# A decoder layer's cross attention: three of six score units get their exponentials head by head on ScalarE

## The chip, the cores and the metric

The kernel runs on one NeuronCore of a Trainium2 chip. A core has engines that run side by side, each with its own instruction stream in fixed order: TensorE (PE, matrix products into PSUM), VectorE (DVE), ScalarE (ACT), GpSimd (POOL) and the queue engine SyncE (SP), which here only issues DMAs. They meet through semaphores. The metric is the device time of the whole program in microseconds (us).

## What is computed

One post-norm decoder layer in float32 for 32 batches of 112 tokens, width 256, 16 heads of 16; the context has 375 tokens per batch. The part that matters here is the cross attention. Its softmax runs over axis 1, the queries, and not over the context:

```python
q = (queries @ Wq + bq).reshape(N, L, H, D)
k = (keys @ Wk + bk).reshape(N, S, H, D)
v = (values @ Wv + bv).reshape(N, S, H, D)
sm = jnp.einsum('nlhd,nshd->nlhs', q, k) / math.sqrt(D)
sm = jax.nn.softmax(sm, axis=1)
attn = jnp.einsum('nlhs,nshd->nlhd', sm, v).reshape(N, L, H * D)
return attn @ Wo + bo
...
x = _layernorm(x + self_attention(x))
x = _layernorm(x + cross_attention(x, ctx, ctx))
x = _layernorm(x + ffn(x))
```

So for each context token and head there is a maximum over 112 queries, an exponential of (score - maximum), and a sum over the same 112 queries.

## The kernel before, in words

The program has three parts one after the other: the feed-forward weights are quantised, then `attention` treats the 32 batches (self attention, cross attention, two layer norms), then the feed-forward part runs over all batches. The change is in `attention`.

**Pipeline.** The batches go through a software pipeline of seven stages. One step of each engine's program works on up to seven batches, n0 (oldest) to n6 (newest). The steps run from i = -6 to 31; in the 26 steps i = 0 to 25 all stages are present (22 of them in a hardware loop of 11 pairs). The order inside a step is written out by hand for each engine, in the functions `step` under `block.tensor`, `block.vector`, `block.scalar` and `block.gpsimd`.

**Units.** The cross scores of one batch are six units, C0 to C5: unit u = (t, c) takes eight heads (t = 0 or 1) and a third of the context (125 tokens, c = 0 to 2). A unit is a tile of 125 partitions (context tokens) by 8 heads x 112 queries = 896 columns, in one of two PSUM slots `score`. `SLOT_USES` fixes the turn: slot 0 takes C4, C5, C1, C2; slot 1 takes S1, C0, S0, C3 (S0 and S1 are the self attention's scores). `wait_slot` makes PE wait until the exponentials of the slot's previous tenant are done.

**A unit's way through the engines**, before:

1. PE `cross_scores` (L1062): six matmuls (L1002).
2. DVE `max_cross` (L744): negated maximum per head, 125x8, into `nmax_c` (L747).
3. PE `transpose_max` (L1071): `nmax_c` transposed into the PSUM tile `maxT` (L1074).
4. ACT `copy_max` (L564): copy to `nmaxT` (L567).
5. PE `shift` (L1076): two selector matmuls add the negated maxima onto the scores in PSUM (L1080).
6. ACT `exp_cross` (L558): one exponential over 125x896 (L561) into `Px`.
7. DVE `sum_cross` (L725): the sums per head into `Zc` (L729); `reciprocal_cross` (L731), then `normalise_values` (L735), which multiplies the values by the reciprocals into `Vn` (L740).
8. PE `cross_values` (L1084): products into `outX` (L1091).

The self attention goes another way: `exp_self` (L546) takes eight exponentials of 112x112, one per head, each with its own bias (the negated maximum) and the sum in ACT's accumulator (L554).

**Around the change.** In an ACT step, `even_cross` (L623, on `outX` after C5's products) stands ahead of `exp_cross(n3, 1)`, behind which come `even_self(n4, 1)` and `exp_self(n5, 0)`. `copy_x1T` stands ahead of `exp_cross(n3, 3)`, and `hi_queries_cross` (tile `Qx_hi`, L573) behind it. On DVE `lo_with_bias` (L758, `Qx_lo`, L763) follows `Qx_hi`; on POOL `block_diagonal` (L482, `Qbd` and `Kbd`, L485) follows that, in a fixed order with `inverse_root` (L503, `rstd`, L506), which needs DVE's `add_eps` (L837, `vare`, L839). In the PE steps the order is: output projection of n0, self keys, shift of C3, ..., C4, ..., S1, ..., C5, ..., C0, ..., transposed maxima of C0, ..., C1, ..., products of C5, ..., C2, ..., C3, ..., transposed maxima of C3.

Of the kernel before, what the change touches and what calls it, by code (L numbers as in the profile page):

```python
# [33 lines left out]
SP = S + 1  # L34
NU = KT * NC
QW = QUAD * L
HALF_ROWS = QUAD * HD
# [52 lines left out]
class Batch:  # L90
# [21 lines left out]
    def loads(self):  # L112

        fixed = 16 * (self.off // 2 + 1)
        return self.pair * 16 + fixed if self.looped else fixed

    def first_fills(self, use):
# [207 lines left out]
def attention(nc, a, ident, x2T_all, xmax_all, x2_dram, constants):  # L325
    with ExitStack() as ctx:
# [38 lines left out]
        x1b = [sb(f"x1b{p}", [L, D]) for p in range(2)]  # L365
        nmax_c = [sb(f"nmax_c{p}", [C, P]) for p in range(2)]
        nmaxT = [sb(f"nmaxT{p}", [P, SP // NC + 1], F32R) for p in range(2)]
        Px = [sb(f"Px{p}", [C, OCT, L]) for p in range(2)]
# [30 lines left out]
        scores_c, nmax_c_done, nmaxT_done = sem("scores_c"), sem("nmax_c_done"), sem("nmaxT_done")  # L399
        nmaxT_copied, shifted, exp_c = sem("nmaxT_copied"), sem("shifted"), sem("exp_c")  # L400
        z_c, rz_c, vn_done, av_done = sem("z_c"), sem("rz_c"), sem("vn_done"), sem("av_done")
# [136 lines left out]
        def _(act):  # L538
# [18 lines left out]

            def exp_cross(n, u):  # L558
                act.wait_ge(shifted, n.times(NU, u + 1))
                wait(act, av_done, n.times(NU, u - 1))  # L560
                act.activation(Px[u % 2][:].rearrange("s (q h) l -> s q (h l)", q=2),  # L561
                               score[SLOT_OF[f"C{u}"]][0:C, :, 0:QW], ACT.Exp).then_inc(exp_c, 1)

            def copy_max(n, u):  # L564
                act.wait_ge(nmaxT_done, n.times(NU, u + 1))
                wait(act, shifted, n.times(NU, u - 1))
                act.activation(nmaxT[u % 2][:, 0:C], maxT[:, 0:C], ACT.Copy).then_inc(nmaxT_copied, 1)  # L567

# [72 lines left out]
            def step(n0, n1, n2, n3, n4, n5, n6):  # L641
                if n4:
                    copy_probs(n4, 0)
                if n2:
                    copy_max(n2, 4)
                    exp_cross(n2, 4)
# [7 lines left out]
                if n2:  # L654
                    copy_max(n2, 5)
                if n4:
                    copy_probs(n4, 2)
                    hi_context(n4, 0)
                if n2:
                    exp_cross(n2, 5)  # L660
                if n3:
                    copy_max(n3, 0)
                if n4:
                    even_self(n4, 0)
                if n3:
                    exp_cross(n3, 0)
                if n4:
                    hi_context(n4, 1)
                    copy_probs(n4, 3)
                if n3:  # L670
                    copy_max(n3, 1)
                if n1:
                    copy_x2T(n1)
                if n2:
                    even_cross(n2)
                if n3:
                    exp_cross(n3, 1)
                if n4:
                    even_self(n4, 1)
                if n5:  # L680
                    exp_self(n5, 0)
                if n3:
                    copy_max(n3, 2)
                if n4:
                    hi_keys_cross(n4, 0)
                if n3:
                    exp_cross(n3, 2)
# [4 lines left out]
                if n3:  # L692
                    copy_max(n3, 3)
                if n6:
                    hi_keys_self(n6)
                if n4:
                    copy_x1T(n4)
                if n3:
                    exp_cross(n3, 3)
                if n4:  # L700
                    hi_queries_cross(n4)
# [3 lines left out]
        def _(dve):  # L705
# [38 lines left out]
            def max_cross(n, u):  # L744
                dve.wait_ge(scores_c, n.times(NU, u + 1))
                wait(dve, nmaxT_done, n.times(NU, u - 1))
                dve.tensor_reduce(nmax_c[u % 2][:, 0:OCT].rearrange("s (q h) -> s q h", q=2),  # L747
                                  score[SLOT_OF[f"C{u}"]][0:C, :, 0:QW].rearrange("s q (h l) -> s q h l", h=QUAD),
                                  AX.X, ALU.max, negate=True).then_inc(nmax_c_done, 1)

# [110 lines left out]
            def step(n0, n1, n2, n3, n4, n5, n6):  # L861
# [9 lines left out]
                if n3:  # L871
                    normalise_values(n3, 2)
                    max_cross(n3, 4)
                    sum_cross(n3, 3)
                if n5:
# [30 lines left out]
                if n5:  # L906
                    lo_context(n5, 0)
                if n3:
                    sum_cross(n3, 5)
                if n5:  # L910
# [31 lines left out]
                if n5:  # L942
                    residual(n5, 0)
                if n4:
                    sum_cross(n4, 1)
                if n5:
# [20 lines left out]
        def _(pe):  # L967
# [103 lines left out]
            def transpose_max(n, u):  # L1071
                pe.wait_ge(nmax_c_done, n.times(NU, u + 1))
                wait(pe, nmaxT_copied, n.times(NU, u))
                pe.transpose(maxT[:, 0:C], nmax_c[u % 2][:], ident[0:C, 0:C]).then_inc(nmaxT_done, 1)  # L1074

            def shift(n, u):  # L1076

                pe.wait_ge(nmaxT_copied, n.times(NU, u + 1))
                for q in range(2):
                    ins = pe.matmul(score[SLOT_OF[f"C{u}"]][0:C, q, 0:QW], nmaxT[u % 2][:, 0:C],  # L1080
                                    sel[:, q * QW:(q + 1) * QW], start=False, stop=True, skip_group_check=True)
# [59 lines left out]
            def step(n0, n1, n2, n3, n4, n5, n6):  # L1141
                if n0:
                    project_out_cross(n0)
                if n4:
                    project_T(n4, "Ks", w["aWk"], xT, "xT")
                if n1:
                    shift(n1, 3)
                if n2:
# [23 lines left out]
                if n4:  # L1172
                    project_T(n4, "Qs", w["aWq"], xT, "xT")
                if n1:
                    transpose_max(n1, 5)
# [5 lines left out]
                if n1:  # L1181
                    shift(n1, 5)
                if n3:
# [12 lines left out]
                if n4:  # L1196
                    self_scores(n4, 0)
                if n2:
                    transpose_max(n2, 1)
# [4 lines left out]
                if n2:  # L1204
                    shift(n2, 1)
                if n3:
# [19 lines left out]
                if n2:  # L1226
                    cross_values(n2, 1)
                    transpose_max(n2, 3)
            iterations(pe, step)


# [606 lines left out]
```

## Time and profile before

| what | value |
|---|---|
| time, median of 3 runs (lowest to highest) | 1400.16 us (1396.43 to 1400.56) |
| time of the profiled execution | 1398.15 us |
| its span in the profile | 1396.4 us |
| busy share of the span: PE, DVE, ACT, POOL | 88%, 83%, 62%, 28% |

The shares are over the whole program. A stage's own limit is read from a stretch of it: each engine's busy time there, then what each engine waits for at the places where it does wait, and the start times of one step side by side. A row of the timeline gives an instruction's start and duration, and in brackets how long the engine was idle ahead of it and who released it. Back-to-back instructions of one engine overlap in the rows, so the time that one takes from its engine is the distance from its start to the next one's start, which is shorter than its duration.

### The profile page before, as it was taken

The numbers are of one execution on the slowest core, as the hardware profiler recorded it, in microseconds if no ns is written. First come the engines' busy times: TensorE is split into PE (matmuls) and PEld (weight loads), VectorE is DVE, ScalarE is ACT, GpSimd is POOL, SyncE is SP. The second block draws the span as 40 slices with busy tenths as digits, with TensorE's granted clock in tenths as the row PEclk, the third lists the DMA queues.
The fourth block names the chain that finished last, engine by engine and source line by source line (L and its number), as shares of the span: only waits on it lengthen the run. The fifth ranks groups of instructions, "written<-read, shape, count | busy, mean of one in ns | idle before, by whom it ended". The sixth has DMA issues, their size and how long they took to land. (4 is left out here: it accounts for less than half of the span.)

```text
span 1396.4 us, 28360 instructions
## 1 busy us (share of the span) xinstructions
PE 1226.5 (88%) x8850; PEld 897.2 (64%) x8850; DVE 1159.4 (83%) x2358; ACT 859.7 (62%) x2306; POOL 396.4 (28%) x463
## 2 busy tenths in 40 slices
PE   1689999999999999999999999999858878596776
PEld 1466666666666666666666666666527766496776
DVE  6369999999999999999999999999853468868787
ACT  2366666666666666666666666666424479786443
POOL 0233322234322234322234322233100000000887
PEclk9999999999999999999999999999969989798898
DMA  5100000000000000000000000000000000000222
GB/s 159 39 19 16 19 28 25 18 21 18 18 27 22 18 21 18 18 28 21 18 21 18 18 29 21 19 19 5 7 7 1 0 0 0 0 1 8 62 69 72
DMA packets 35042, 33.07 MB, mean 24 GB/s; under 512 B 4148, under 2 KB 34604, under 8 KB 34988
## 3 DMA queue, kind: packets, MB, share of 16 engines
q1 hardware_dynamic: 32704, 31.50, 7.3%
q10 hardware_dynamic: 2284, 0.89, 0.3%
q8 instruction: 30, 0.49, 0.1%
q14 instruction: 24, 0.20, 0.0%
HBM read 25.04 MB, written 7.34 MB: 23 GB/s over the span
## 5 line engine op out<-in xcount | busy, mean ns | idle before, releaser
L561 ACT ACTIVATE Px<-score 125x896 f32<-125x896 f32 x192 | 176.2, 918 | 128.1 <-PE score L1080 66.7
L747 DVE TENSOR_REDUCE nmax_c<-score 125x8 f32<-125x896 f32 x192 | 208.3, 1085 | 5.6 <-PE score L1002 5.1
L729 DVE TENSOR_REDUCE Zc<-Px 125x8 f32<-125x896 f32 x192 | 206.6, 1076 | 7.3 <-ACT Px L561 3.8
L554 ACT ACTIVATE Ps<-score,nmax_s 112x112 f32<-112x112 f32 x512 | 173.1, 377 | 3.9 <-DVE nmax_s L754 3.9
L506 POOL TENSOR_TENSOR rstd<-vare,half 112x1 f32<-112x1 f32 x64 | 35.1, 548 | 473.6 <-DVE vare L839 473.6
L1080 PE MATMUL score<-sel,nmaxT 128*125 128x448 f32 x384 | 125.1, 407 | 1.8 <-ACT nmaxT L567 1.8
L554 ACT ACTIVATION_READ_ACCUMULATOR Ps<-score,nmax_s 112x1 f32 x512 | 118.6, 232 | 0.0
L1091 PE MATMUL outX<-Px,Vn 125*32 125x224 f32 x1536 | 113.2, 368 | 2.5 <-DVE Vn L740 2.5
L740 DVE TENSOR_TENSOR Vn<-Vx,rZc 125x128 f32<-125x128 f32 x192 | 112.8, 588 | 1.2
L567 ACT ACTIVATE nmaxT<-maxT 128x125 fp32r<-128x125 f32 x192 | 53.5, 279 | 89.2 <-PE maxT L1074 88.9
L1002 PE MATMUL score<-Qbd_hi,KxT_hi 64*125 64x448 f32 x384 | 90.3, 466 | 1.2 <-ACT Px L561 1.2
L485 POOL TENSOR_TENSOR Qbd_hi<-Qx_hi,mask 128x448 fp32r<-128x448 f32 x64 | 59.7, 933 | 103.2 <-DVE Qx_lo L763 102.2
L1074 PE MATMUL maxT<-ident,nmax_c 125*128 125x125 f32 x192 | 59.7, 311 | 31.2 <-DVE nmax_c L747 31.2
L593 ACT ACTIVATE PsT<-work 112x448 f32<-112x448 f32 x128 | 69.5, 543 | 25.9 <-PE work L1126 24.5
L1126 PE MATMUL work<-ident,Ps 112*112 112x112 f32 x512 | 75.5, 270 | 3.6 <-ACT Ps L554 2.0
L1074 PEld LDWEIGHTS maxT<-ident,nmax_c 125*128 125x128 f32 x192 | 27.3, 142 | 79.6 <-DVE nmax_c L747 57.4
L1126 PEld LDWEIGHTS work<-ident,Ps 112*112 112x112 f32 x512 | 51.5, 134 | 36.4 <-DVE KxT_lo L776 10.1
L1080 PEld LDWEIGHTS score<-sel,nmaxT 128*125 128x125 f32 x384 | 57.5, 187 | 24.9 <-ACT nmaxT L567 17.4
L754 DVE TENSOR_REDUCE nmax_s<-score 112x8 f32<-112x896 f32 x64 | 69.1, 1080 | 3.3 <-PE score L1002 3.3
L1002 PE MATMUL score<-Qbd_hi,KxT_lo 64*125 64x448 f32 x384 | 71.2, 364 | 0.0
L1002 PE MATMUL score<-Qbd_lo,KxT_hi 64*125 64x448 f32 x384 | 71.1, 365 | 0.0
L1667 POOL MEMSET fhalf<- 112x1 f32 x1 | 0.1, 98 | 249.6 <-POOLq L1544 249.6
(252 smaller groups left out, 3588.1 us busy)
## 6 DMA issues: line engine op xcount, KB each, us to landing
ctx_in<-in_ctx SPq DMA_DIRECT2D x32, 375.0 KB
x_in<-in_x SPq DMA_DIRECT2D x32, 112.0 KB, 2.0
x_scratch<-x SPq DMA_DIRECT2D x32, 112.0 KB, 5.4
x2T_all<-x_scratch SPq DMA_DIRECT2D x32, 112.0 KB, 2.0
out<-x2T_all SPq DMA_DIRECT2D x32, 112.0 KB, 1.9
raw_w_up<-in_w_up SPq DMA_DIRECT2D x1, 768.0 KB, 5.6
raw_w_down<-in_w_down SPq DMA_DIRECT2D x1, 768.0 KB, 7.2
raw_w_gate<-in_w_gate SPq DMA_DIRECT2D x1, 768.0 KB, 9.6
```

The source lines that it names most:

```text
L554: ins = act.activation(Ps[:, g, :], score[slot][0:L, h // QUAD, (h % QUAD) * L:(h % QUAD + 1) * L], ACT.Exp, bias=nmax_s[:, g:g + 1], accu ...
L561: act.activation(Px[u % 2][:].rearrange("s (q h) l -> s q (h l)", q=2), score[SLOT_OF[f"C{u}"]][0:C, :, 0:QW], ACT.Exp).then_inc(exp_c, 1)
L593: act.activation(dst, work[b][0:rows_, 0:cols], ACT.Copy).then_inc(drained[b], 1)
L729: dve.tensor_reduce(Zc[p][:], Px[p][:], AX.X, ALU.add).then_inc(z_c, 1)
L740: dve.tensor_tensor(Vn[p][:], Vx[n.par][:, c, P * t:P * (t + 1)].rearrange("s (h e) -> s h e", h=OCT), rZc[p][:].rearrange("s (h o) -> s h ...
L747: dve.tensor_reduce(nmax_c[u % 2][:, 0:OCT].rearrange("s (q h) -> s q h", q=2), score[SLOT_OF[f"C{u}"]][0:C, :, 0:QW].rearrange("s q (h l) ...
L754: dve.tensor_reduce(nmax_s[:, OCT * t:OCT * (t + 1)].rearrange("s (q h) -> s q h", q=2), score[SLOT_OF[f"S{t}"]][0:L, :, 0:QW].rearrange(" ...
L1002: ins = pe.matmul(dst[:, q, 0:QW], lhs[a][rows, t, cols], rhs[b][rows, t].rearrange("p h l -> p (h l)"), start=(first and i == 0), stop=(i ...
L1074: pe.transpose(maxT[:, 0:C], nmax_c[u % 2][:], ident[0:C, 0:C]).then_inc(nmaxT_done, 1)
L1080: ins = pe.matmul(score[SLOT_OF[f"C{u}"]][0:C, q, 0:QW], nmaxT[u % 2][:, 0:C], sel[:, q * QW:(q + 1) * QW], start=False, stop=True, skip_g ...
L1091: ins = pe.matmul(outX[32 * g:32 * (g + 1), t, :], Vn[u % 2][:, 2 * g:2 * g + 2, :].rearrange("s h e -> s (h e)"), Px[u % 2][:, 2 * g:2 * ...
L1126: ins = pe.transpose(b[0:L, h * L:(h + 1) * L], Ps[:, QUAD * j + h, :], ident[0:L, 0:L])
```

## The change

The units are split: C1, C3 and C5 (`BY_HEAD`) lose the steps 3, 4, 5 and the DVE sum, and their exponentials are eight ACT instructions of 125x112, one per head, with the negated maximum as bias and the sum in the accumulator (`exp_by_head`). C0, C2 and C4 (`SHIFTED`) go as before. The maxima of the by-head units go to tiles of their own (`nmax_h`); counts and buffer parities of the shifted units follow their own numbering. The by-head exponentials stand where the single ones stood. Nothing else is reordered.

```diff
+BY_HEAD = (1, 3, 5)
+SHIFTED = tuple(u for u in range(NU) if u not in BY_HEAD)
...
+            def exp_by_head(n, u):
+                i = BY_HEAD.index(u)
+                act.wait_ge(nmax_h_done, n.times(NBH, i + 1))
+                wait(act, av_done, n.times(NU, u - 1))
+                maxima, sums = nmax_h[(n.par * NBH + i) % 2], Zc[u % 2]
+                for h in range(OCT):
+                    ins = act.activation(Px[u % 2][:, h, :],
+                                         score[SLOT_OF[f"C{u}"]][0:C, h // QUAD, (h % QUAD) * L:(h % QUAD + 1) * L],
+                                         ACT.Exp, bias=maxima[:, h:h + 1], accum_out=sums[:, h:h + 1])
+                ins.then_inc(exp_c, 1)
...
             def reciprocal_cross(n, u):
-                dve.wait_ge(z_c, n.times(NU, u + 1))
+                if u in BY_HEAD:
+                    dve.wait_ge(exp_c, n.times(NU, u + 1))
+                else:
+                    dve.wait_ge(z_c, n.shifts(SHIFTED.index(u) + 1))
...
-                if n3:
-                    copy_max(n3, 1)
                 if n1:
                     copy_x2T(n1)
                 if n2:
                     even_cross(n2)
                 if n3:
-                    exp_cross(n3, 1)
+                    exp_by_head(n3, 1)
```

The other two copies on ACT, the sums of units 1, 3 and 5 on DVE (three lines), and their transposes and shifts on PE (three of each) are taken out of the steps in the same way.

On ACT, the stretch around unit 1's exponential, before (`work` is a PSUM bank, L554 is `exp_self`, L626 `even_cross`):

```order
L567 ACTIVATE nmaxT1<-maxT 128x125
L433 REGISTER_ALU
L604 ISA
L604 ACTIVATE x2T_all<-work1 128x2x112
L142 REGISTER_ALU
L626 ACTIVATE evenX<-outX,even_odd 128x224
L561 ACTIVATE Px1<-score0 125x896
L433 REGISTER_ALU
L620 ACTIVATE evenT<-work0,even_odd 128x112
L548 REGISTER_ALU
L554 ACTIVATE Ps,Zs<-score1,nmax_s 112x112 x8
```

and the same stretch after:

```order
L631 ISA
L631 ACTIVATE x2T_all<-work1 128x2x112
L651 REGISTER_ALU
L155 REGISTER_ALU
L653 ACTIVATE evenX<-outX,even_odd 128x224
L579 ACTIVATE Px1,Zc1<-score0,nmax_h0 125x112 x8
L447 REGISTER_ALU
L647 ACTIVATE evenT<-work0,even_odd 128x112
L562 REGISTER_ALU
L568 ACTIVATE Ps,Zs<-score1,nmax_s 112x112 x8
```

The copy of the maxima is gone, and one instruction between `evenX` and `evenT` has become eight. On PE, the stretch from the output projection (`xWo`) to C4's first product, before:

```order
L1039 MATMUL work<-xWo,OxT 112x256 x2
L142 ISA
L1031 MATMUL work<-xT,aWk 128x112 x4
L1078 ISA
L1080 MATMUL score<-sel,nmaxT 125x448 x2
L1019 REGISTER_ALU
L142 REGISTER_ALU
L1011 MATMUL work<-ident,x 128x112 x2
L142 REGISTER_ALU
L1002 MATMUL score<-Qbd_hi,KxT_hi 125x448 x2
```

and after:

```order
L1065 MATMUL work<-xWo,OxT 112x256 x2
L155 ISA
L1057 MATMUL work<-xT,aWk 128x112 x4
L1045 REGISTER_ALU
L155 REGISTER_ALU
L1037 MATMUL work<-ident,x 128x112 x2
L155 ISA
L1028 MATMUL score<-Qbd_hi,KxT_hi 125x448 x2
```

C3's shift has gone from between the self keys and the transpose of x1; the rest stands in the same order.

## Rows read from the trace of the kernel before

**Rows 1.** Busy time of the engines in three stretches; x is the count, PEclk the granted clock.

```profile
core 0: us, PE busy (x) PEld busy (x) DVE busy (x) ACT busy (x) POOL busy (x), PEclk, DMA share, GB/s
400.00:600.00 200.00, 193.73 (x1546) 132.73 (x1546) 186.76 (x408) 134.24 (x436) 67.31 (x83) 1.00 0.07 21
980.00:1010.00 30.00, 25.67 (x197) 15.94 (x189) 26.85 (x59) 13.41 (x29) 5.48 (x7) 1.00 0.02 6
```

**Rows 2.** Timeline of PE, one step; start, duration, engine, line, instruction, idle before.

```profile
517.59 1.03 PE L1039 MATMUL work<-xWo,OxT 128*112 128x256 f32 x4
...
519.26 0.65 PE L1080 MATMUL score<-sel,nmaxT 128*125 128x448 f32 x2
519.75 0.36 PE L1011 MATMUL work<-ident,x 112*128 112x112 f32 x2
...
533.09 0.33 PE L1074 MATMUL maxT<-ident,nmax_c 125*128 125x125 f32 x1 [0.86 <-DVE nmax_c L747]
...
534.16 0.66 PE L1080 MATMUL score<-sel,nmaxT 128*125 128x448 f32 x2
...
537.46 0.59 PE L1091 MATMUL outX<-Px,Vn 125*32 125x224 f32 x8
...
540.10 0.46 PE L1002 MATMUL score<-Qbd_hi,KxT_hi 64*125 64x448 f32 x2
...
547.29 0.33 PE L1074 MATMUL maxT<-ident,nmax_c 125*128 125x125 f32 x1
547.45 1.03 PE L1039 MATMUL work<-xWo,OxT 128*112 128x256 f32 x4
```

**Rows 3.** Timeline of DVE: C3's sum.

```profile
542.40 1.08 DVE L729 TENSOR_REDUCE Zc<-Px 125x8 f32<-125x896 f32 x1
```

**Rows 4.** The page's group for the copies; busy us, mean ns of one, idle before.

```profile
L567 ACT ACTIVATE nmaxT<-maxT 128x125 fp32r<-128x125 f32 x192 | 53.5, 279 | 89.2 <-PE maxT L1074 88.9
```

**Rows 5.** Timeline of ACT: first and last head of `exp_self`, and on to C5.

```profile
526.02 0.35 ACT L554 ACTIVATE Ps<-score,nmax_s 112x112 f32<-112x112 f32 x1
...
528.58 0.24 ACT L554 ACTIVATION_READ_ACCUMULATOR Ps<-score,nmax_s 112x1 f32 x1
528.67 0.61 ACT L638 ACTIVATE KxT_hi<-work,xbk 128x375 fp32r<-128x375 f32 x1
...
531.60 0.92 ACT L561 ACTIVATE Px<-score 125x896 f32<-125x896 f32 x1
```

**Rows 6.** Timeline of ACT at the exponentials of C1.

```profile
538.20 0.45 ACT L626 ACTIVATE evenX<-outX,even_odd 128x224 f32<-128x224 f32 x1 [0.17 <-PE outX L1091]
538.69 0.92 ACT L561 ACTIVATE Px<-score 125x896 f32<-125x896 f32 x1
```

**Rows 7.** Timeline of ACT around the exponentials of C3.

```profile
519.53 0.60 ACT L573 ACTIVATE Ks_hi<-work,abk 128x112 fp32r<-128x112 f32 x2 [1.47 <-PE work L1031]
520.15 0.36 ACT L593 ACTIVATE x1T<-work 128x224 f32<-128x224 f32 x1
520.40 0.91 ACT L561 ACTIVATE Px<-score 125x896 f32<-125x896 f32 x1
522.38 0.60 ACT L573 ACTIVATE Qx_hi<-work,xbq 128x112 fp32r<-128x112 f32 x2 [1.07 <-PE work L1031]
```

**Rows 8.** Timeline of DVE behind `Qx_hi`.

```profile
523.88 0.96 DVE L740 TENSOR_TENSOR Vn<-Vx,rZc 125x128 f32<-125x128 f32 x1
524.76 1.08 DVE L754 TENSOR_REDUCE nmax_s<-score 112x8 f32<-112x896 f32 x1
...
530.40 1.63 DVE L740 TENSOR_TENSOR Vn<-Vx,rZc 125x128 f32<-125x128 f32 x1
```

**Rows 9.** Timeline of POOL behind `Qx_lo`.

```profile
523.76 0.93 POOL L485 TENSOR_TENSOR Qbd_hi<-Qx_hi,mask 128x448 fp32r<-128x448 f32 x1 [3.18 <-DVE Qx_lo L763]
...
525.98 0.55 POOL L506 TENSOR_TENSOR rstd<-vare,half 112x1 f32<-112x1 f32 x1 [0.35 <-DVE vare L839]
...
530.95 0.93 POOL L485 TENSOR_TENSOR Qbd_lo<-Qx_lo,mask 128x448 fp32r<-128x448 f32 x1
```

More of the change, by code:

```diff
@@ L35 @@
 NU = KT * NC
+BY_HEAD = (1, 3, 5)
+SHIFTED = tuple(u for u in range(NU) if u not in BY_HEAD)
+NSH = len(SHIFTED)
+NBH = len(BY_HEAD)
 QW = QUAD * L
@@ L115, in loads, with shifts, exps @@
         return self.pair * 16 + fixed if self.looped else fixed
+    def shifts(self, i):
+        return self.times(NSH, i)
+    def exps(self, place):
+        ahead, i = divmod(place, NBH)
+        return self.times(NU, NU * ahead + BY_HEAD[i] + 1)
     def first_fills(self, use):
@@ L366, in attention @@
         nmax_c = [sb(f"nmax_c{p}", [C, P]) for p in range(2)]
+        nmax_h = [sb(f"nmax_h{p}", [C, OCT]) for p in range(2)]
         nmaxT = [sb(f"nmaxT{p}", [P, SP // NC + 1], F32R) for p in range(2)]
@@ L399, in attention @@
         scores_c, nmax_c_done, nmaxT_done = sem("scores_c"), sem("nmax_c_done"), sem("nmaxT_done")
-        nmaxT_copied, shifted, exp_c = sem("nmaxT_copied"), sem("shifted"), sem("exp_c")
+        nmaxT_copied, shifted, exp_c, nmax_h_done = (sem(n) for n in ("nmaxT_copied", "shifted", "exp_c", "nmax_h_done"))
         z_c, rz_c, vn_done, av_done = sem("z_c"), sem("rz_c"), sem("vn_done"), sem("av_done")
@@ L556, in exp_self, with exp_shifted @@
                 ins.then_inc(exp_s, 1)
-            def exp_cross(n, u):
-                act.wait_ge(shifted, n.times(NU, u + 1))
+            def exp_by_head(n, u):
[8 more added lines that the diff above has]
+                ins.then_inc(exp_c, 1)
+            def exp_shifted(n, u):
+                act.wait_ge(shifted, n.shifts(SHIFTED.index(u) + 1))
                 wait(act, av_done, n.times(NU, u - 1))
@@ L564, in copy_max @@
             def copy_max(n, u):
-                act.wait_ge(nmaxT_done, n.times(NU, u + 1))
-                wait(act, shifted, n.times(NU, u - 1))
-                act.activation(nmaxT[u % 2][:, 0:C], maxT[:, 0:C], ACT.Copy).then_inc(nmaxT_copied, 1)
+                i = SHIFTED.index(u)
+                act.wait_ge(nmaxT_done, n.shifts(i + 1))
+                wait(act, shifted, n.shifts(i - 1))
+                act.activation(nmaxT[(n.par * NSH + i) % 2][:, 0:C], maxT[:, 0:C], ACT.Copy).then_inc(nmaxT_copied, 1)
             def hi_with_bias(n, use, dst, bias, done):
@@ L645, in step @@
                     copy_max(n2, 4)
-                    exp_cross(n2, 4)
+                    exp_shifted(n2, 4)
                 if n4:
@@ L659, in step @@
                 if n2:
-                    exp_cross(n2, 5)
+                    exp_by_head(n2, 5)
                 if n3:
@@ L665, in step @@
                 if n3:
-                    exp_cross(n3, 0)
+                    exp_shifted(n3, 0)
                 if n4:
@@ L686, in step @@
                 if n3:
-                    exp_cross(n3, 2)
+                    exp_shifted(n3, 2)
                 if n5:
@@ L691, in step @@
                     copy_xT(n6)
-                if n3:
-                    copy_max(n3, 3)
                 if n6:
@@ L698, in step @@
                 if n3:
-                    exp_cross(n3, 3)
+                    exp_by_head(n3, 3)
                 if n4:
@@ L745, in max_cross @@
                 dve.wait_ge(scores_c, n.times(NU, u + 1))
-                wait(dve, nmaxT_done, n.times(NU, u - 1))
-                dve.tensor_reduce(nmax_c[u % 2][:, 0:OCT].rearrange("s (q h) -> s q h", q=2),
+                if u in BY_HEAD:
+                    i = BY_HEAD.index(u)
+                    wait(dve, exp_c, n.exps(i - 2))
+                    dst, done = nmax_h[(n.par * NBH + i) % 2][:], nmax_h_done
+                else:
+                    i = SHIFTED.index(u)
+                    wait(dve, nmaxT_done, n.shifts(i - 1))
+                    dst, done = nmax_c[(n.par * NSH + i) % 2][:, 0:OCT], nmax_c_done
+                dve.tensor_reduce(dst.rearrange("s (q h) -> s q h", q=2),
                                   score[SLOT_OF[f"C{u}"]][0:C, :, 0:QW].rearrange("s q (h l) -> s q h l", h=QUAD),
-                                  AX.X, ALU.max, negate=True).then_inc(nmax_c_done, 1)
+                                  AX.X, ALU.max, negate=True).then_inc(done, 1)
             def max_self(n, t):
@@ L873, in step @@
                     max_cross(n3, 4)
-                    sum_cross(n3, 3)
                 if n5:
@@ L1071, in transpose_max @@
             def transpose_max(n, u):
-                pe.wait_ge(nmax_c_done, n.times(NU, u + 1))
-                wait(pe, nmaxT_copied, n.times(NU, u))
-                pe.transpose(maxT[:, 0:C], nmax_c[u % 2][:], ident[0:C, 0:C]).then_inc(nmaxT_done, 1)
+                i = SHIFTED.index(u)
+                pe.wait_ge(nmax_c_done, n.shifts(i + 1))
+                wait(pe, nmaxT_copied, n.shifts(i))
+                pe.transpose(maxT[:, 0:C], nmax_c[(n.par * NSH + i) % 2][:], ident[0:C, 0:C]).then_inc(nmaxT_done, 1)
             def shift(n, u):
-                pe.wait_ge(nmaxT_copied, n.times(NU, u + 1))
+                i = SHIFTED.index(u)
+                pe.wait_ge(nmaxT_copied, n.shifts(i + 1))
                 for q in range(2):
-                    ins = pe.matmul(score[SLOT_OF[f"C{u}"]][0:C, q, 0:QW], nmaxT[u % 2][:, 0:C],
+                    ins = pe.matmul(score[SLOT_OF[f"C{u}"]][0:C, q, 0:QW], nmaxT[(n.par * NSH + i) % 2][:, 0:C],
                                     sel[:, q * QW:(q + 1) * QW], start=False, stop=True, skip_group_check=True)
@@ L1145, in step @@
                     project_T(n4, "Ks", w["aWk"], xT, "xT")
-                if n1:
-                    shift(n1, 3)
                 if n2:
@@ L1180, in step @@
                     transpose_ctx(n3, 0)
-                if n1:
-                    shift(n1, 5)
                 if n3:
@@ L1203, in step @@
                     cross_values(n1, 5)
-                if n2:
-                    shift(n2, 1)
                 if n3:
@@ L1227, in step @@
                     cross_values(n2, 1)
-                    transpose_max(n2, 3)
             iterations(pe, step)
```

10 lines of the change are left out of this document (removed).

## The prediction

> **What bounds the kernel now.** I read the stretches first [rows 1]: from 400 to 600 us PE is busy for 193.7 of 200 us, DVE for 186.8 and ACT for 134.2, and PE has the full clock. Then the timeline of one PE step [rows 2]: PE waits for another engine at one place, 0.86 us for the maxima of C0. So a step is PE's own work plus that one wait. It is 29.86 us long, from the output projection at 517.59 to the next at 547.45. I cut it where the change can bite: **A** from the output projection to C0's transposed maxima (533.09), 15.50 us; **B** from there to the products of C5 (537.46), 4.37 us; **C** to the first matmul of C2 (540.10), 2.64 us; **D** to the next output projection, 7.35 us [rows 2].
>
> **What the change takes away.** On PE a shift is worth 519.75 - 519.26 = 0.49 us and a transposition of maxima 547.45 - 547.29 = 0.16 us [rows 2]; three of each are 1.95 us per step. On DVE a sum lasts 1.08 us [rows 3]; neighbours overlap, so I take 1.0 us, three are 3.0 us. ACT loses three copies of 0.28 us [rows 4]. If PE's work were all that counts, the step would fall to 27.9 us.
>
> **What it adds.** The nearest thing to the new exponentials is `exp_self`: eight heads of 112 columns, bias from a tile, sum in the accumulator, source in PSUM. From the first head to the next other instruction it takes 528.67 - 526.02 = 2.65 us of ACT, and its result is complete at 528.58 + 0.24 = 528.82, 2.80 us after the start [rows 5]. One exponential over the whole tile is complete 0.92 us after its start [rows 6]. So per by-head unit the exponentials end 1.88 us later from the same start. The new heads differ in having 125 partitions for 112; I take the same time for both. As a check of the total: ACT was busy for 134.2/200 x 29.86 = 20.0 us per step [rows 1]; three times (2.65 - 0.9) more, less three copies, gives about 25 us. ACT still has room on average, so its total is not the limit. What counts is where the longer blocks stand in its fixed order, and who waits behind them.
>
> Here the skill speaks for a lower price. By the row, head follows head every 2.65/8 = 0.33 us [rows 5]. The Trainium skill, page "ScalarE: Activation LUTs", section "What ACT_TABLE_LOAD costs", gives an ACTIVATE with a bias pointer about 280 ns plus 0.833 ns per column, with about 93 ns overlap of neighbours. By it a head would come every 0.28 us (an estimate), and eight heads would take 2.24 us, with no reading of the accumulator counted. The rows have such a reading behind the head, so I hold to 0.33 us; a lower price is a rival below.
>
> **Segment C (unit 1), the largest term.** C2 lies in slot 0 behind C1, so PE may not begin C2 before C1's exponentials are complete. ACT takes them behind `even_cross`, which waits for C5's products. From the start of the products to the start of the exponentials it is 538.69 - 537.46 = 1.23 us [rows 2, 6]. Before, they were complete at 539.61 and PE came to C2 at 540.10: 0.49 us to spare, so hidden. Now C takes 1.23 + 2.80 + about 0.05 to get going = 4.08 us for 2.64: **+1.44 us**. PE's own work in C is shorter by a shift, which only lengthens its wait.
>
> **Segment A (unit 3).** The exponentials of C3 stand behind `copy_x1T`. With C3's shift gone from PE, x1's transposition is ready 0.49 us earlier, but ACT is in the two instructions of `Ks_hi` (from 519.53) until about 520.02, so the eight heads start at 520.27 for 520.40 and hold ACT until 522.92. Behind them is `Qx_hi`, which started at 522.38 after 1.07 us of waiting for PE [rows 7]: 0.54 us later. What hangs on it is tight: `Qx_lo` on DVE; POOL's `Qbd_hi`, which waited for it; `Vn` on DVE, stretched to 0.96 us beside that; the self attention's maximum; `vare`; POOL's `rstd`, which waited 0.35 us for it, and then six `Kbd` and `Qbd` products up to 531.88. The next `Vn` takes 1.63 us and ends at 532.03, with the last of them [rows 8, 9]; C0's maximum follows, and PE has waited 0.86 us for it [rows 2]. So the shifts of C3 and C5, gone from A, only lengthen this wait, and A grows by the delay of `Qx_hi`: **+0.54 us**. The sum of C3, which DVE no longer does ahead of `Qx_lo`, gives nothing, since `Qx_lo` waits for `Qx_hi` anyway.
>
> **Segment B (unit 5).** One transposition less is -0.16 us. Against it stands the copy of C0's maxima on ACT, now behind C5's eight heads. The self maximum ended at 525.84, 0.18 us before `exp_self` began [rows 5, 8]; 0.54 us late, it moves `exp_self` and what follows on ACT by 0.36 us, C5's exponentials too, from 531.60 to 531.96 [rows 5]. Its heads then hold ACT until 534.61. C0's maxima are transposed by 533.63 + 0.33 = 533.96; the copy waits 0.65 us and ends at 534.89, and C0's shift, due at 533.63 + 534.16 - 533.09 = 534.70 [rows 2], slips by about **0.20 us**. B: +0.04 us. C1 needs slot 0 free, which by then it is.
>
> **Segment D.** One transposition less, -0.16 us; the self attention's output projection waits about 0.05 us more for `even_self`, now behind C1's heads. D: **-0.11 us**. DVE lacks a sum here and is done sooner, but PE is not waiting for it.
>
> **Sum.** 1.44 + 0.54 + 0.04 - 0.11 = +1.91 us, a step of 31.8 us. All stages are present in 26 steps: 50 us. The steps of filling have some of the longer blocks; in draining, chains get shorter by a transposition, a copy, a shift and a sum and longer by 1.88 us. I put both ends together at +1. The profiled execution took 1398.15 us, 2 us below the median of 1400.16, and gives 1398.15 + 51 = **1449 us**.
>
> For TensorE's clock I charge nothing: where PE is busy for 25.7 of 30 us its granted clock is still full, 2.4 GHz [rows 1], and in the new step it has about 28 us of 31.8. The Trainium skill, "TensorE: Matmul & The Clock Gate", section "What's actually happening", has the clock at half when the engine has been idle; if the new waits did that, the sum would be too low, and the row speaks against it.
>
> **Rivals.**
> - *Cheaper heads, or a chain in A that is shorter than I think.* If eight heads hold ACT for 2.24 us (the bound would be 0.28 us per head, as a head's own instruction lasts 0.35 us and the reading might hide), C grows by 1.03, A by 0.13, and B and D change by -0.3: +0.9 us per step, 23 us, **1421 us**. For it: DVE has 3 us less to do in a step. Against: the spacing in [rows 5]. 0.16.
> - *More waits.* ACT's later finish costs again: `Qx_hi` late by more than 0.54 us, a `Vn` that meets another POOL product (1.63 us against 0.96 in [rows 8]), or slot 1 freed too late for S1. About 1 us more per step: **1475 us**. For it: three engines are tight; against: each of these has a few tenths to spare. 0.12.
> - *Faster.* PE's 1.95 us per step come through in 30 steps: **1340 us**; with half of them 1370 us. The place is C2's wait for slot 0. It decides where C1's heads are complete within 0.92 us of their start (the spare 0.49 us goes with PE's own shift), or start 1.9 us earlier. Nothing in ACT's order lets them: `even_cross` is still ahead. 0.07.
> - *No change.* The losses in C and A are just met by gains that I put at nothing: 1400 us. 0.05.
>
> **How the numbers follow.** The forecast has 0.60, the rivals 0.16, 0.12, 0.07 and 0.05. The likeliest case gives 1449. The range goes from 1420 (cheap heads) to 1476 (more waits), leaves out the last two cases and the outer part of the first two, and holds about 0.8. A change of less than 0.3%, 4.2 us, can't be told from none. Faster: 0.07; same: 0.05; slower: 0.88.
>
> **What would show it.** In the profile after: a step of 31.8 us; a new wait of PE ahead of C2, about 1.8 us per step; the wait for C0's maxima grown from 0.86 to 2.0 to 2.5 us; in 400 to 600 us PE busy at 85 to 90%, DVE near 80%, ACT near 78%; a head every 0.33 us; `Qx_hi` directly behind the heads of C3. I am wrong if C2 doesn't wait for ACT, if heads come at another distance than 0.33 us, or if the step is below 30 us.

## The result, and the profile after

The changed kernel takes 1527.35 us (median of 4, 1526.94 to 1529.48), the kernel before 1399.3 us in the same runs: a ratio of 1.092 (95% interval 1.090 to 1.094), 128 us slower. The direction is that of the forecast of 1449 us, the size is far outside its range. The profiled execution has a span of 1525.3 us. Behind the last `evenX` of the attention part the two kernels have about the same time left (365.0 and 364.7 us), so the whole loss lies ahead of it.

Busy time in the stretch of [rows 1], kernel after:

```profile
core 0: us, PE busy (x) PEld busy (x) DVE busy (x) ACT busy (x) POOL busy (x), PEclk, DMA share, GB/s
400.00:600.00 200.00, 178.31 (x1314) 118.46 (x1312) 148.24 (x341) 142.28 (x622) 58.52 (x72) 0.93 0.06 18
```

PE is busy 89% for 97%, DVE 74% for 93%, ACT 71% for 67%. The third number from the end, PEclk, is 0.93 and was 1.00: TensorE was at 1.2 GHz in a part of this stretch, and was not before. What PE waits for, same stretch (total us, times, longest):

```profile
PE score L1028 <- ACT Px L579: 8.4, 5, 1.7
...
PE maxT L1101 <- DVE nmax_c L778: 6.5, 6, 1.2
...
PE score L1085 <- ACT Px L579: 3.0, 6, 0.5
```

The first is C2's wait for the heads of C1, new; the second the wait of [rows 2] for C0's maxima; the third, also new, S1's wait for the heads of C3, which hold its slot. One step on PE:

```profile
507.85 1.12 PE L1065 MATMUL work<-xWo,OxT 128*112 128x256 f32 x4
...
524.01 0.33 PE L1101 MATMUL maxT<-ident,nmax_c 125*128 125x125 f32 x1 [0.96 <-DVE nmax_c L778]
...
525.46 0.67 PE L1108 MATMUL score<-sel,nmaxT 128*125 128x448 f32 x2
...
528.67 0.59 PE L1119 MATMUL outX<-Px,Vn 125*32 125x224 f32 x8
...
532.60 0.47 PE L1028 MATMUL score<-Qbd_hi,KxT_hi 64*125 64x448 f32 x2 [1.67 <-ACT Px L579]
...
533.52 1.90 PE L1065 MATMUL work<-aWo,attnT 128*112 128x256 f32 x4
534.86 0.88 PE L1019 MATMUL work<-ctxT_hi,xWk_hi 128*128 128x376 f32 x1
...
541.53 1.12 PE L1065 MATMUL work<-xWo,OxT 128*112 128x256 f32 x4
```

By the cuts of the prediction: A 16.16 us, B 4.66, C 3.93, D 8.93. A, B and C are near the forecast of 16.04, 4.41 and 4.08. D should be 7.24. The four matmuls of the self attention's output projection (`aWo`), right behind the new wait, take 1.90 us. One step earlier they took 1.12:

```profile
501.47 1.12 PE L1065 MATMUL work<-aWo,attnT 128*112 128x256 f32 x4
```

The granted clock of two stretches, the wait itself and what follows it:

```profile
core 0: us, PE busy (x) PEld busy (x) DVE busy (x) ACT busy (x) POOL busy (x), PEclk, DMA share, GB/s
528.70:532.60 3.90, 2.23 (x24) 1.19 (x23) 2.50 (x4) 3.55 (x19) 0.00 (x0) 1.00 0.20 70
...
532.60:537.00 4.40, 4.37 (x16) 3.52 (x17) 3.13 (x9) 2.89 (x17) 0.00 (x0) 0.63 0.00 0
```

While PE waits the clock is full; in the work after it, it is down for a part of the time. It does not fall at every wait: behind the C2 wait that ended at 500.55 it stayed up, and in the step after this one it fell behind the wait for C0's maxima (557.70). Of the 23 whole steps between 200 and 1000 us, 20 have a slow D, 12 a slow B, and none has neither.

ACT around C3's heads, C0's copy and C1's heads:

```profile
510.61 0.37 ACT L579 ACTIVATE Px<-score,nmax_h 125x112 f32<-125x112 f32 x1
...
513.25 0.67 ACT L600 ACTIVATE Qx_hi<-work,xbq 128x112 fp32r<-128x112 f32 x2
...
525.07 0.34 ACT L594 ACTIVATE nmaxT<-maxT 128x125 fp32r<-128x125 f32 x1
...
529.41 0.45 ACT L653 ACTIVATE evenX<-outX,even_odd 128x224 f32<-128x224 f32 x1 [0.17 <-PE outX L1119]
529.75 0.35 ACT L579 ACTIVATE Px<-score,nmax_h 125x112 f32<-125x112 f32 x1
...
532.30 0.25 ACT L579 ACTIVATION_READ_ACCUMULATOR Px<-score,nmax_h 125x1 f32 x1
```

The heads of C3 hold ACT for 513.25 - 510.61 = 2.64 us, and `Qx_hi` follows with no idle time; the heads of C1 are complete 532.55 - 529.75 = 2.80 us after their start, as `exp_self` in [rows 5]. They start 1.08 us after C5's products and not 1.23.

### The profile page after: what moved, and what is told of

Its sections match the earlier page's. It is cut to its first block and busy times, and to the rows that moved or that the text cites. A ratio compares the mean times of both kernels' runs of the same rounds, so it can differ in the third digit from the quotient of the medians.

```text
span 1525.3 us, 28904 instructions
## 1 busy us (share of the span) xinstructions
PE 1266.5 (83%) x8562; PEld 908.7 (60%) x8562; DVE 1073.6 (70%) x2262; ACT 1004.0 (66%) x3650; POOL 396.2 (26%) x463
## 3 DMA queue, kind: packets, MB, share of 16 engines
HBM read 25.04 MB, written 7.34 MB: 21 GB/s over the span
## 5 line engine op out<-in xcount | busy, mean ns | idle before, releaser
L579 ACT ACTIVATE Px<-score,nmax_h 125x112 f32<-125x112 f32 x768 | 260.1, 378 | 2.8 <-DVE nmax_h L778 2.7
L579 ACT ACTIVATION_READ_ACCUMULATOR Px<-score,nmax_h 125x1 f32 x768 | 178.5, 232 | 0.0
L587 ACT ACTIVATE Px<-score 125x896 f32<-125x896 f32 x96 | 88.2, 919 | 117.0 <-PE outX L1119 58.6
L568 ACT ACTIVATION_READ_ACCUMULATOR Ps<-score,nmax_s 112x1 f32 x512 | 128.2, 250 | 0.0
L778 DVE TENSOR_REDUCE nmax_h<-score 125x8 f32<-125x896 f32 x96 | 104.2, 1085 | 33.5 <-PE score L1028 33.1
L750 DVE TENSOR_REDUCE Zc<-Px 125x8 f32<-125x896 f32 x96 | 103.5, 1078 | 5.1 <-ACT Px L587 3.0
L778 DVE TENSOR_REDUCE nmax_c<-score 125x8 f32<-125x896 f32 x96 | 104.0, 1083 | 3.7 <-PE score L1028 3.7
L1028 PEld LDWEIGHTS score<-Qbd_hi,KxT_hi 64*125 64x125 f32 x384 | 37.1, 190 | 107.8 <-ACT Px L579 60.7
L834 DVE SCALAR_TENSOR_TENSOR sumT<-work,even_odd,evenT 128x112 f32<-128x112 f32 x64 | 21.4, 334 | 80.3 <-ACT evenT L647 80.3
L807 DVE SCALAR_TENSOR_TENSOR KxT_lo<-work,xbk,KxT_hi 128x375 fp32r<-128x375 f32 x64 | 38.9, 608 | 54.7 <-ACT KxT_hi L665 54.7
```

The source lines that it names most:

```text
L568: ins = act.activation(Ps[:, g, :], score[slot][0:L, h // QUAD, (h % QUAD) * L:(h % QUAD + 1) * L], ACT.Exp, bias=nmax_s[:, g:g + 1], accu ...
L579: ins = act.activation(Px[u % 2][:, h, :], score[SLOT_OF[f"C{u}"]][0:C, h // QUAD, (h % QUAD) * L:(h % QUAD + 1) * L], ACT.Exp, bias=maxim ...
L750: dve.tensor_reduce(Zc[p][:], Px[p][:], AX.X, ALU.add).then_inc(z_c, 1)
L778: dve.tensor_reduce(dst.rearrange("s (q h) -> s q h", q=2), score[SLOT_OF[f"C{u}"]][0:C, :, 0:QW].rearrange("s q (h l) -> s q h l", h=QUAD ...
L1028: ins = pe.matmul(dst[:, q, 0:QW], lhs[a][rows, t, cols], rhs[b][rows, t].rearrange("p h l -> p (h l)"), start=(first and i == 0), stop=(i ...
```

## The experiments

**Theory K**: the loss has two parts of about the same size. One is the longer chain that the prediction worked out, some 2.1 us per step. The other is TensorE's clock, which falls behind the lengthened waits. **Rival R**: ScalarE's load and the waits for it are the whole loss, and the low clock stands beside them at no cost.

The table has, for each kernel, the median distance between the four cuts over the steps from 200 to 1000 us (starts in PE's timeline, as above), and the mean step. For the steps I took the starts of `evenX` on ACT: two in a row are one step apart; the mean is over 26 of them. Where the clock falls in some steps only, a median is that of the commoner kind.

| kernel | A | B | C | D | mean step | PEclk, 200 to 1000 us | time |
|---|---|---|---|---|---|---|---|
| before | 15.50 | 4.38 | 2.63 | 7.36 | 29.87 | 1.00 | 1399 |
| after | 16.16 | 5.71 | 3.92 | 8.88 | 34.04 | 0.93 | 1527 |
| after, three waits filled | 16.17 | 4.56 | 3.92 | 7.30 | 31.94 | 1.00 | 1464 |
| unit 1 alone | 15.50 | 4.27 | 3.92 | 7.47 | 31.62 | 0.99 | 1451 |
| unit 3 alone | 16.17 | 4.38 | 2.63 | 7.19 | 30.37 | 1.00 | 1416 |
| unit 5 alone | 15.50 | 4.77 | 2.63 | 7.34 | 30.70 | 0.98 | 1430 |

**The waits filled with work.** Matmuls whose result nobody reads, in a free part of the PSUM bank of `maxT`:

```diff
+            def keep_busy(count):
+                for _ in range(count):
+                    pe.matmul(maxT[0:C, P:BANK], sel[:, 0:C], sel[:, 0:BANK - P], start=True, stop=True)
...
+                    keep_busy(9)
                     cross_scores(n2, 2)
...
+                    keep_busy(5)
                     transpose_max(n2, 0)
...
+                    keep_busy(2)
                     transpose_max(n1, 4)
```

> The changed kernel with extra matmuls on TensorE whose result nobody reads: nine (128x384 columns, some 0.16 us each) ahead of C2, five ahead of the transposed maxima of C0, two ahead of the transposed maxima of C4. They lie inside waits of 1.67, 0.96 and 0.5 us, so they should not lengthen a step by themselves. Theory K (half of the loss is TensorE's clock, which falls behind the new waits, and half is the longer chain): the granted clock in 400 to 600 us goes from 0.93 back to 1.00, every step is 32.0 us, and the time is 1399 + 29 x 2.1 = about 1460 us. Rival R (the whole loss is waiting for ScalarE, and the low clock stands beside it without costing anything): 1527 us, as the changed kernel.

1463.62 us (ratio 1.046, 1.044 to 1.048): PE has some 2.5 us more to do in each step, and the kernel is 64 us faster than the changed one. The clock:

```profile
400.00:600.00 200.00, 195.09 (x1481) 133.69 (x1477) 157.73 (x360) 153.23 (x679) 64.05 (x79) 1.00 0.06 18
```

From 200 to 1000 us every step is between 31.8 and 32.1 us, and was 32.0 to 36.2 us. R is out. Of the 128 us, 64 are the clock and 64 the chain.

**Only one of the places filled.**

> The changed kernel with the nine unread matmuls ahead of C2 only; the waits for the maxima of C0 and for S1's slot stay empty. In the changed kernel the segment behind the C2 wait (D) is 8.66 us on average for 7.30 at full clock, and the segment behind the C0 wait (B) 5.39 for 4.56. Theory K1 (each wait pulls the clock down for the work right behind it): D goes to 7.30, B stays near 5.4, 1527 - 29 x 1.36 = about 1488 us. Rival K2 (the clock answers to the emptiness of the whole step, and one filled wait is enough): 1464 us, as with all three filled.

1502.85 us (ratio 1.075, 1.071 to 1.080). D has a median of 7.31 us and B stays at 5.77.

> The changed kernel with the five unread matmuls ahead of the transposed maxima of C0 only. Theory K1: B goes to 4.56, D stays near 8.7, 1527 - 29 x 0.83 = about 1503 us. Rival K2: 1464 us.

1492.77 us (ratio 1.068, 1.066 to 1.070). B has a median of 4.60 us, D stays at 8.86. The clock falls for the work behind that wait which is left empty (K1), and stays full behind the filled one. The two gains, 24.5 and 34.6 us, make up 59 of the 64 us; but by the means of D and B I had expected the larger one for C2's wait and it went the other way. With one place filled the other one meets the low clock in a different number of steps: a slow B in 16 of 23 with C2's wait filled (12 without), a slow D in 15 of 23 with C0's wait filled (20 without). So, in the one profiled execution of each, filling one place also acts on the other, which K1 does not have, and the two shares can't be read as prices of the places.

**One unit at a time.** The edit is `BY_HEAD = (1,)`, `(3,)` or `(5,)`, with the other units' transposes, copies, shifts and sums where they stood.

> Only unit 1 takes its exponentials per head; units 0, 2, 3, 4, 5 are shifted as before. Theory K (slot 0's wait for C1's heads is the largest term of the chain, +1.4 us per step, and this wait is also what pulls the clock down in most steps): a step of 31.0 us where the clock is full, wait ahead of C2 about 1.2 to 1.7 us, some episodes of low clock; 1399 + 29 x (1.2 + 1) = about 1463 us, 1435 if the clock stays full. Rival R (the load on ScalarE as a whole counts, whichever unit it is): a third of the loss, 1442 us, and the same for each of the three single-unit kernels.

1451.31 us (ratio 1.037, 1.036 to 1.039). C grows by 1.29 us, and most steps are 31.1 us long; in a third of them the clock falls and they are 32.7.

> Only unit 3 takes its exponentials per head. Theory K: the delay of Qx_hi behind the eight heads costs +0.5 us per step, less one transposition in the last segment (0.16 us): +0.4 us x 29 = 12 us, 1411 us; the wait for C0's maxima grows from 0.86 to about 1.9 us and may pull the clock down, then up to 1440 us. Rival R (load on ScalarE): 1442 us, equal to the other two.

1415.53 us (ratio 1.011, 1.009 to 1.013). A grows by 0.67, D shrinks by 0.17: the step is 30.37 us, always, at full clock.

> Only unit 5 takes its exponentials per head. Theory K: the heads hold ScalarE only until about C0's maxima are transposed, so nothing waits on them; one shift and one transposition less ahead of an existing wait for DVE give nothing: 0 us, 1397 to 1403 us, with the wait for C0's maxima at 1.5 us; if that wait pulls the clock down, up to 1425. Rival R (load on ScalarE): 1442 us.

1429.7 us (ratio 1.022, 1.020 to 1.023), and here theory K missed, with about 0 us expected, 25 if the clock should fall. B grows by 0.39 us, and in 11 of 25 steps the clock falls right behind the wait for C0's maxima:

```profile
516.16 0.47 PE L1121 MATMUL maxT<-ident,nmax_c 125*128 125x125 f32 x1 [1.07 <-DVE nmax_c L791]
516.56 0.98 PE L1141 MATMUL outX<-Px,Vn 125*32 125x224 f32 x8
```

The same products take 0.59 us at full clock. R misses too: the three kernels have about the same load on ScalarE and lose 52, 16 and 30 us, not 43 each. Their steps at full clock are longer than before by 1.28, 0.50 and 0.36 us; together that is 2.14 us, near the 2.07 us of all three units with the waits filled. So the chain's parts add up.

The wait was 0.86 and 0.95 us by turns in the kernel before, where the clock stayed full from 200 to 1000 us, and is 0.96 and 1.07 us by turns here. The longer wait is not the one that counts: the clock also stays up behind 1.08 us and falls behind 0.96 us.

```profile
577.66 0.33 PE L1121 MATMUL maxT<-ident,nmax_c 125*128 125x125 f32 x1 [1.08 <-DVE nmax_c L791]
577.92 0.58 PE L1141 MATMUL outX<-Px,Vn 125*32 125x224 f32 x8
...
607.86 0.33 PE L1121 MATMUL maxT<-ident,nmax_c 125*128 125x125 f32 x1 [0.96 <-DVE nmax_c L791]
608.12 0.89 PE L1141 MATMUL outX<-Px,Vn 125*32 125x224 f32 x8
```

To see whether the loss is the clock, the same kernel with that one wait filled:

> Only unit 5 per head at the old place, with five unread matmuls ahead of the transposed maxima of C0. Without them the time was 1429.7 us, the steps alternate between 30.2 and 31.3 us, and the clock falls in every second step, although TensorE's wait for C0's maxima is 1.07 us and was 0.86 us before the change. Theory K (of the 30 us lost, 0.3 us per step is the copy of C0's maxima behind the heads, and the rest is the clock): every step 30.2 us, clock 1.00, 1399 + 29 x 0.3 = about 1409 us. Rival (the alternation comes from ScalarE's order in the pairs of the loop and not from the clock): 1430 us.

1412.62 us (ratio 1.0095, 1.008 to 1.011), every step 30.0 to 30.4 us. Of what unit 5 cost, 17 us were the clock and 14 us the longer chain: 0.36 us in each step, and the ends.

**Does order or load count?** If the chain through the heads is the cause, moving them in ScalarE's stream must move the time, with the same work on every engine. The edit to the kernel with unit 3 alone (shortened):

```diff
                 if n3:
+                    exp_cross(n3, 3)
                 if n6:
                     hi_keys_self(n6)
                 if n4:
                     copy_x1T(n4)
-                if n3:
-                    exp_cross(n3, 3)
```

> Only unit 3 per head, and its eight heads stand ahead of the self keys' Ks_hi on ScalarE and no longer behind the copy of x1's transpose. ScalarE idled there 1.5 us, and C3's maxima are ready 3 us before. Theory K (segment A is the chain from Qx_hi over POOL to C0's maxima): Qx_hi starts when TensorE has finished its input, one shift (0.49 us) earlier than in the kernel before; A goes from 15.50 to about 15.0, and D loses a transposition (0.16): a step of 29.2 us, 1399 - 28 x 0.65 = about 1381 us. Rival (the chain in A is held by something else, POOL or DVE work that does not move): A stays at 15.5, 1395 us.

1411.79 us (ratio 1.009, 1.007 to 1.0105), against 1415.53: a miss. A is 16.03 us. The timeline of ACT there shows why:

```profile
524.01 0.35 ACT L579 ACTIVATE Px<-score,nmax_h 125x112 f32<-125x112 f32 x1
...
526.66 0.64 ACT L605 ACTIVATE Ks_hi<-work,abk 128x112 fp32r<-128x112 f32 x2
527.14 0.41 ACT L625 ACTIVATE x1T<-work 128x224 f32<-128x224 f32 x1
```

and that of PE:

```profile
527.60 0.59 PE L1176 MATMUL work<-ident,Ps 112*112 112x112 f32 x4 [0.73 <-ACT x1T L625]
```

The heads may start only when the products of C1, which read the same `Px` tile, are done (output projection at 523.87, heads at 524.01). So they end too late for `Ks_hi` and the copy of x1's transpose, and PE waits for that copy: the delay had only changed places.

The same move for C3 together with C1's heads ahead of `even_cross`, in the changed kernel:

> The changed kernel (units 1, 3, 5 per head) with the heads of C3 ahead of Ks_hi and the heads of C1 ahead of the even half of the outputs (even_cross), behind the copy of x2's transpose. Theory K: A falls from 16.17 to about 15.1; C from 3.92 to about 3.45 (even_cross holds ScalarE for 0.34 to 0.49 us); B 4.5, D 7.3: a step of 30.3 us where the clock is full, and less low clock than in the changed kernel since the waits are shorter: 1415 to 1440 us. Rival (ScalarE's load itself is the bound): 1520 us or more, since the load is the same.

1517.01 us (ratio 1.084, 1.078 to 1.091): C fell from 3.92 to 3.50 us as expected, A is 16.03 us as in the kernel above and for the same reason, D rose to 9.34 at the median: DVE's picks of the outputs come after `even_cross`, which is now behind the heads, and PE waits 0.5 us for `attnT`. PE waits at C2 for 1.3 us in place of 1.7, and the clock falls as often. A hit in one term, with a gain of 10 us at the median (its four times reach from 1508 to 1527, so this is hardly clear of noise); the range of 1415 to 1440 was wrong.

**Heads split in two.** Five of C3's heads ahead of `Ks_hi`, three behind the copy of x1's transpose. The edit to the kernel with unit 3 alone (shortened):

```diff
+                if n3:
+                    exp_by_head(n3, 3, range(5))
                 if n6:
                     hi_keys_self(n6)
                 if n4:
                     copy_x1T(n4)
                 if n3:
-                    exp_cross(n3, 3)
+                    exp_by_head(n3, 3, range(5, OCT))
```

> Only unit 3 per head, five of its heads ahead of Ks_hi and three behind the copy of x1's transpose. With all eight ahead, they could start only when AV1's products were done (524.01, the output projection being at 523.87), Ks_hi came 0.8 us late and TensorE waited 0.73 us for the copy of x1's transpose: the wait had only moved. Theory K: five heads (1.65 us) end just when the self keys are ready, three more end before Qx_hi's input: Qx_hi starts 4.3 us after the output projection (4.79 before, 5.27 with eight ahead), A falls from 15.50 to 15.0 us, D by 0.16: a step of 29.2 us, 1381 us. Rival (the chain in A is held by something that does not move with Qx_hi): A at 15.4 or more, 1395 us or more.

**1387.16 us**, ratio 0.991 (0.989 to 0.993): faster than both kernels. Its stretches of ACT and PE:

```profile
545.24 0.60 ACT L607 ACTIVATE Ks_hi<-work,abk 128x112 fp32r<-128x112 f32 x2
545.73 0.36 ACT L627 ACTIVATE x1T<-work 128x224 f32<-128x224 f32 x1
545.97 0.36 ACT L580 ACTIVATE Px<-score,nmax_h 125x112 f32<-125x112 f32 x1
...
547.74 0.60 ACT L607 ACTIVATE Qx_hi<-work,xbq 128x112 fp32r<-128x112 f32 x2 [0.65 <-PE work L1079]
```

```profile
543.21 1.12 PE L1087 MATMUL work<-xWo,OxT 128*112 128x256 f32 x4
```

The expectation was 1381 us. `Qx_hi` starts 4.53 us after the output projection (4.79 before, in [rows 2, 7]) and waits for PE, not for the heads. A is 15.24 us, D 7.18, the step 29.43 with the clock full. A moves with `Qx_hi` one to one in this kernel (0.26 us each), as the prediction's chain has it. The other by-head units, split too:

> Units 1, 3 and 5 per head, all split: unit 3 as in the kernel with unit 3 alone (5 + 3), unit 5 with three heads ahead of the copy of the probabilities (ScalarE idled there 0.9 us) and five at the old place, unit 1 with four heads ahead of the copy of x2's transpose and four behind even_cross. The work of every engine is that of the changed kernel. Theory K (order, not load): A 15.0, B 4.2, C 2.9, D 7.2, a step of 29.3 us, and the waits are short enough for a full clock: 1399 - 28 x 0.6 = 1382 us. Rival (load of ScalarE): 1500 us or more.

1484.76 us (ratio 1.060, 1.056 to 1.064). A is 15.23, as wanted, but C is 4.08, for two waits of PE, 200 to 1000 us:

```profile
PE work L1045 <- ACT x2T_all L638: 25.7, 24, 1.2
...
PE score L1054 <- ACT Px L580: 16.8, 24, 0.7
```

The four heads ahead of the copy of x2's transpose delay that copy, for which the next values' matmuls wait 1.1 us; then come the 0.7 us for the rest of the heads. The clock is at 0.95. My expectation had looked at where the copy stood, and not at what lets the four heads begin. It is not C1's maxima, which DVE had at 544.48 + 1.09 = 545.57, but the products of C5, which read the same `Px` tile, as in the kernel with unit 3's heads early:

```profile
544.48 1.09 DVE L799 TENSOR_REDUCE nmax_h<-score 125x8 f32<-125x896 f32 x1 [0.59 <-PE score L1054]
...
546.16 0.58 PE L1149 MATMUL outX<-Px,Vn 125*32 125x224 f32 x8
546.82 0.35 ACT L580 ACTIVATE Px<-score,nmax_h 125x112 f32<-125x112 f32 x1 [1.28 <-PE outX L1149]
...
548.15 0.37 ACT L638 ACTIVATE x2T_all<-work 128x224 f32 x1
```

> Units 3 and 5 per head, split the same way; unit 1 is shifted as before, so that slot 0 is free in time for C2. Theory K: A 15.0, B 4.2, C 2.64, D 7.2: a step of 29.0 us, 1399 - 28 x 0.9 = 1374 us. Rival: unit 5 gains nothing, 1381 us, as unit 3 alone.

1421.7 us (ratio 1.015, 1.013 to 1.018). Without unit 1, the undisturbed steps are 29.4 us long, no shorter than with unit 3 alone, and in ten others, every second step from 285 to 836 us, C4's shift waits for the copy of C4's maxima, and the clock falls (0.98):

```profile
PE score L1136 <- ACT nmaxT L601: 17.4, 10, 1.9
```

The copy is late because ScalarE stood still for about 2 us just ahead of it, each time at the same instruction and with nothing that the profile shows to wait for ("issue"). No other kernel here has such a stop within the steps; what makes it is open:

```profile
292.36 0.54 ACT L627 ACTIVATE PsT<-work 112x448 f32<-112x448 f32 x1 [2.19 <-issue]
292.80 0.27 ACT L601 ACTIVATE nmaxT<-maxT 128x125 fp32r<-128x125 f32 x1
```

So this time is no test of the order of unit 5's heads. Its undisturbed steps say only that unit 5 gave nothing there.

So order decides more than load: the same work of unit 3 alone has taken 1416, 1412 and 1387 us, and that of units 1, 3 and 5 1527, 1517 and 1485 us. But no kernel with units 1 or 5 in it got below the kernel before, in the orders tried.

## Why the prediction was wrong

- **Segment C**: right in mechanism and nearly in size. 4.08 us predicted, 3.92 measured, with unit 1 alone too. The 0.16 us too much is the start of the heads, 1.08 us after C5's products and not 1.23. `evenX` starts 0.74 us after them in both kernels; the heads start 0.34 us behind it, where the single exponential started 0.49 us behind it. The likely reason is C1's shift, which a by-head unit does not have: in the kernel before, whose row follows, it ended at 537.98 + 0.67 = 538.65, just ahead of the exponential's start at 538.69. No run tells this apart.

```profile
537.98 0.67 PE L1080 MATMUL score<-sel,nmaxT 128*125 128x448 f32 x2
```

- **Price of a head**: 0.33 us predicted, 0.33 measured, and 2.80 us to completion. The Trainium skill, page "ScalarE: Activation LUTs", section "What ACT_TABLE_LOAD costs", gives by its figures 0.28 us (an estimate); the trace has a reading of the accumulator behind each head, 0.23 us long, and its 0.33 us decide.
- **Segment A**: 16.04 predicted, 16.16 measured. `Qx_hi` starts 5.40 us after the output projection for 4.79 before: 0.61 us later and not 0.54, since the heads of C3 start 2.76 us after it and not 2.68. That is 0.07 of the 0.12 us. The new wait of S1 for the heads of C3 (0.5 us), named among the rivals as "slot 1 freed too late", took place and can be worth the other 0.05 us at most.
- **Segment B**: 4.41 predicted, 4.56 measured with full clock. Behind C0's transposed maxima the shift starts 1.45 us later in the step shown (525.46 - 524.01), for 1.07 before: it slips by 0.38 us, and not by 0.20. With the waits filled it is 1.27 us in about half of the steps, the 0.20 predicted, and 1.44 us in the rest. And from the shift to C5's products it is 3.21 us for 3.30, so the transposition less gave 0.09 us and not 0.16. With unit 5 alone nothing is late ahead of C5's heads, and the prediction's way of counting gives 0.37 us (heads to 531.60 + 2.65 = 534.25, copy to 534.53, shift due at 534.16); B grew by 0.36 with the wait filled. The mechanism holds.
- **Segment D**: 7.24 predicted, 7.30 with full clock.
- **Sum of the chain**: 31.8 us per step predicted, 31.94 measured. But "all stages are present in 26 steps" and "both ends together at +1" were too small: with the waits filled the first 28 steps were all about 31.8 us or longer, the first `evenX` came 4.8 us later (124.7 for 119.9 us), and of the last steps one had 3.3 us more. The chain came to 64 us, not 51.
- **The step that failed** is the one sentence "For TensorE's clock I charge nothing". Its row was a stretch of 30 us with 86% busy and full clock. A mean over a stretch does not say whether the clock stays up behind a given gap, and I took the statement of the Trainium skill, "TensorE: Matmul & The Clock Gate", section "What's actually happening", that the clock is at half when the engine has been idle, as contradicted by it. Behind the waits of 1.67 and 0.96 to 1.2 us the granted clock was down in each step at one place or at both, and it cost 64 us. The page pointed the right way; but with no wait of PE above 1.7 us in those steps, and a full clock in unit 3's kernel with waits of up to 1.2 us, no run here shows when its rule sets in. The trace of the kernel before had the row to ask for, just behind my stretch: where the attention part drains, waits of 1.01 and 1.18 us came close together, and the next shift took 1.11 us for 0.67.

```profile
1010.55 0.47 PE L1002 MATMUL score<-Qbd_hi,KxT_hi 64*125 64x448 f32 x2 [1.01 <-ACT Px L561]
...
1012.62 0.47 PE L1074 MATMUL maxT<-ident,nmax_c 125*128 125x125 f32 x1 [1.18 <-DVE nmax_c L747]
1013.46 1.11 PE L1080 MATMUL score<-sel,nmaxT 128*125 128x448 f32 x2 [0.37 <-ACT nmaxT L567]
```

```profile
core 0: us, PE busy (x) PEld busy (x) DVE busy (x) ACT busy (x) POOL busy (x), PEclk, DMA share, GB/s
1012.60:1016.00 3.40, 3.02 (x13) 1.59 (x17) 1.45 (x3) 0.28 (x1) 0.00 (x0) 0.50 0.02 5
```

I named the clock as something that would make the sum too low, and gave it neither a chance nor a price; it needed both, with the work that stands behind the two waits, in B and D, at half speed as its bound. The upper end, 1476 us, was made of other waits, and so the range missed.

- **What the profile was to show**: a new wait ahead of C2, 1.8 us predicted, 1.67 measured; PE at 85 to 90%, 89%; ACT near 78%, 71%; DVE near 80%, 74%. The last two are low since the step is longer than thought (and ACT's work was summed up a little high: 20.0 + 3 x 1.75 - 3 x 0.28 is 24.4 us per step, not 25). The wait for C0's maxima was to grow to 2.0 to 2.5 us and is 0.96 to 1.2: the freed PE time came out at other waits ahead of it, S1's, and one of 0.23 us for `KxT_lo`, one of 0.29 us for `PsT`.
- **Rivals**: "faster", "no change" and "cheaper heads" are out. "More waits" had the right sign and, with 1475 us, less than half of the rest of the loss, by another mechanism.

What stays open: what makes the clock fall at one wait and not at the next. Unit 3 alone has waits of up to 1.2 and 0.5 us in each step and a full clock from 200 to 1000 us; unit 5 alone has one of 0.96 or 1.07 us and a low clock in 11 of 25 steps. The length of the wait is not the whole of it, and the runs don't say what the rest is.

## What to carry to other kernels

Where TensorE is busy nearly all the time, a new wait can cost twice, as here: by its length, and by the work behind it at half the clock. Give the second part a price and a chance too. A test that costs one run is to fill the wait with matmuls whose result is not used; if the time falls and the granted clock rises, it was the clock. And when one long instruction becomes a row of short ones on an in-order engine, look at who stands behind it there, and cut the row at that place: five heads before and three after made a loss of 1.1% into a gain of 0.9%. Then ask what lets the moved part begin, and who waits next: the moves that left this out mostly shifted the delay.

## What the runs showed of the hardware

TensorE finished sooner with more work in its stream: sixteen matmuls per step that nobody needs took 64 us (4.2%) off the kernel, and in 200 to 1000 us the granted clock was 1.00 (2.4 GHz) in place of 0.93. The four matmuls of a projection took 1.12 us at full clock and 1.45 to 2.05 us where the clock was down for a part of them or for all. Eight exponentials of 112 columns with accumulator took 2.64 us of ScalarE with 125 partitions and 2.65 us with 112. `Vn` on DVE still took 0.96 and 1.70 to 1.86 us beside POOL's instructions in the changed kernel (0.28 us elsewhere), for 0.96 and 1.63 us in [rows 8]: relief of DVE did not shorten that stretch.
